# Layer-1 attention: normalise the probabilities on POOL before they are turned, one output product for a pair of heads

## The chip, the cores and the metric

One core of one Trainium2 chip runs the whole program. The metric is the device time of one execution in microseconds. The kernel before took 1533.4 us (median of three runs, 1531.64 to 1533.47). The engines are written as the profile writes them: PE is TensorE (with PEld for its weight loads), DVE is VectorE, ACT is ScalarE, POOL is GpSimd, SP is SyncE.

## The reference

The program computes a whole two-layer block on x of 2 x 1024 x 128: layer 0 has a test-time-training attention and a second attention with a mixture of experts; layer 1 has the causal attention below and a mixture of 8 experts with top 2. The change touches only the layer-1 attention: 16 heads of 64 dimensions, sequence 1024, batch 2.

```
k = einsum('ihd,bpd->biph', W_K, x)
q = einsum('ihd,bpd->biph', W_Q, x)
v = einsum('ihd,bpd->biph', W_V, x)
scores = einsum('biph,biqh->biqp', k, q)
mask = tril(ones((S, S)))
scores_masked = tril(scores) - 10000000000.0 * (1.0 - mask)
attn = softmax(scores_masked / sqrt(64), axis=-1)
z = einsum('biph,biqp->biqh', v, attn)
z_flat = transpose(z, (0, 2, 1, 3)).reshape(B, S, -1)
out = einsum('df,bqf->bqd', W_O, z_flat)
```

Its result is added to x, together with that of the experts.

## The kernel before

The attention stage runs from about 794 us (first projections) to 1375 us (first product of the experts). It works in 16 **rounds**; a round is one pair of heads of one batch element. Within a round `u` from 0 to 15 names a row tile `i = u // 2` of 128 queries and a head `h = u % 2` of the pair; the tile has `i + 1` blocks of 128 keys, so a row of probabilities has 128 to 1024 columns. Because all four engines work on different steps at once, the order of each is written out as a list of short words. A word with `'` belongs to the round before the current one, a word with `+` to the next. The words are:

- PE: `q k v` projections of 512 columns (L2044, L2052); `S` scores of one `u`, from the split parts KA, KB and QA (L2002, L2003); `T` turns (transposes) the probabilities of one `u`, up to four blocks at a time (L2010); `pv` multiplies them with V for one of three groups of tiles (0 to 3, 4 and 5, 6 and 7; L2024); `w` is the output product (L2037).
- DVE: `mx` masks the scores and takes the row minimum of their negative, in two records (L1516); `ql` writes the low part of Q, two operations with both inputs in SBUF (L1552); `kd` copies the high part of K to the other half of the partitions, two operations (L1555); `x` adds the output product to X (L1560, L1568); `gate` is the routing of the experts.
- ACT: `ex` is the exponential of a row, with its sum into SM (L1023).
- `tc`, `zc`, `vc`, `qr`, `kr` move results of PE out of PSUM, on ACT or DVE as the lists say.
- POOL: `qh`, `kh` write the high parts of Q and K (two casts each, L836, L842), `kl` the low part of K (two subtractions, L848).

PN holds the probabilities of three `u` at a time (`NPROB`), so `ex` of `u` waits for the turning of `u - 3`. S waits for the exponential that frees its PSUM banks: from `u = 10` that is `u - 2`. The ring of three PSUM banks takes the results of `T`, `w`, `q`, `k`, `v` in PE's order; each waits until the third one before it has been moved out.

The probabilities stay undivided until the very end. Z1 holds, for 128 queries, both heads of the pair in its 128 partitions (64 each). The sums of the two heads differ, so the output product is made per head: WOZ holds each head's 64 rows of W_O with zeros in the other 64, `w` makes four products of 128 columns (two tiles, two heads), and `x` multiplies each with 1/sum of its row and adds it to X. WOZ is cleared on POOL after `kl1` of the first round (L853) and filled by two DMAs. A round has 16 such products on PE, and 4 reciprocals of 4 columns and 16 multiply-adds of 128 columns on DVE. Before the first round POOL does, in this order, `kh1 kl1`, the clearing, `qh1 kh0 qh0 kl0`, and S0 waits for `ql0`, `kd0` and `kl0`.

Of the kernel before, what the change touches and what calls it, by code (L numbers as in the profile page):

```python
# [11 lines left out]
ALU = mybir.AluOpType  # L12
# [66 lines left out]
def program(nc, x_in, w0_in, w1_in, out):  # L79
    with ExitStack() as ctx:  # L80
# [123 lines left out]
        WOZ = sb("WOZ", [P, H1, D])  # L204
        NPROB = 3
# [253 lines left out]
        PAIRS = range(0, TB, 2)  # L459
# [18 lines left out]
        PE1 = steps1("T14.1' S0 T13.1' S1 T13.0' T15.0' w0' S2 T14.0' S3 T15.1' S4 k1+ T0.0 S5 k0+ S6 T1.0 w4' S7 T3.0 "  # L478
                     "T2.0 pv2' T5.0 T4.0 T6.0 S8 q1+ T7.0 S9 w2' q0+ S10 T8.0 T8.1 S11 pv0 T9.0 T9.1 S12 T11.1 T10.1 "
                     "v1 S13 v0+ T10.0 T11.0 S14 gate0+ T12.0 w6' T12.1 S15 pv1")  # L480
        DVE1 = steps1("gate1 mx5 x4' mx7 tc2.0 tc5.0 tc4.0 mx8 tc7.0 mx9 x2' mx10 mx11 ql0+ mx12 vc1 mx13 tc10.0 mx14 "
                     "gate0+ kd0+ mx15 x6' tc12.1 kd1+ mx1+ mx0+ x0 zc1 mx2+ mx3+ ql1+ mx4+ mx6+")
        ACT1 = steps1("tc13.1' tc13.0' tc15.0' ex0 ex1 tc14.0' tc15.1' gate0 ex2 kr1+ tc0.0 ex3 kr0+ tc1.0 ex4 tc3.0 "
                     "ex6 ex5 ex7 tc6.0 qr1+ ex8 ex9 zc2' qr0+ tc8.1 tc8.0 ex10 ex11 tc9.0 tc9.1 tc11.1 tc10.1 ex12 "
                     "vc0+ tc11.0 ex13 zc0 tc12.0 ex14 ex15 tc14.1")
        POOL1 = steps1("kh1 kl1 qh1 kh0 qh0 kl0")

        def rounds(steps):
# [10 lines left out]
        score_max, low_q, dup_k, out_added = (  # L499
            sem("l1_max"), sem("l1_q_low"), sem("l1_k_doubled"), sem("l1_out_added"))  # L500
# [4 lines left out]
        high_q, high_k, low_k = sem("l1_q_high"), sem("l1_k_high"), sem("l1_k_low")  # L505
# [4 lines left out]
        def counts(steps, **signals):  # L510
            n = {}
            for item, r in rounds(steps):
                if item[0] == "gate":
                    continue
                s = signals[item[0]]
                if item[0] == "x":
                    for part in ("r", 0, 1, 2):
                        n[s.name] = n.get(s.name, 0) + 1
                        done1[("x", item[1], part), r] = (s, n[s.name])
# [149 lines left out]
        def _(sp):  # L669
# [25 lines left out]
        def _(pool):  # L695
# [160 lines left out]
            after(pool, POOL1[-1][0], ROUNDS - 1)  # L856
            after(pool, ("kl", 0), ROUNDS - 1)
            after(pool, ("qh", 1), ROUNDS - 1)
# [22 lines left out]
        def _(act):  # L881
# [132 lines left out]
            for item, r in rounds(ACT1):  # L1014
# [17 lines left out]
                elif kind == "zc":  # L1032
                    g = item[1]
                    after(act, ("pv", g), r)
                    for i in PAIRS:
                        if GROUP_OF[i] == (g + 1) % 3:
                            after(act, ("w", i), r - 1 if g < 2 else r)
# [30 lines left out]
        def _(dve):  # L1068
# [436 lines left out]
            for item, r in rounds(DVE1):  # L1505
# [644 lines left out]
```

## Time and profile before

| | |
|---|---|
| median of three runs | 1533.4 us |
| the profiled execution | 1532.58 us |
| its span | 1530.8 us |
| PE busy | 1412.0 us (92%) |
| DVE busy | 1097.4 us (72%) |
| ACT busy | 786.8 us (51%) |
| POOL busy | 239.9 us (16%) |
| one round in the middle (1054.14 to 1088.21) | 34.07 us |

The shares are averages over all stages. What counts for this change is the stretch from 794 to 1375 us. A matrix product of f32 by f32 leaves two records on PE and its records overlap, so the pace of PE is read from the starts of successive groups and not from the durations.

### The profile page before, as it was taken

To read this page: it belongs to the slowest core of one execution; us is meant where nothing else is said; L and a number is where in the kernel's file an instruction comes from. 1 tells how busy PE (TensorE), PEld (TensorE's weight loads), DVE (VectorE), ACT (ScalarE), POOL (GpSimd) and SP (SyncE) were. 2 spreads that over 40 slices of the span, in tenths; PEclk is the share of its full clock that TensorE was granted. 3 is DMA by queue.
4 is the path that set the end of the run, shared out by engine and by line. 5 is a ranking of instruction groups with operands and counts; after the bars stand their busy time and mean duration, and the time that the engine had idled before them with its cause. 6 is when DMAs were issued, how large, how long until landed. Compare 5 with 4: busy or idle time off the path is not lost.

```text
span 1530.8 us, 30652 instructions
## 1 busy us (share of the span) xinstructions
PE 1412.0 (92%) x9716; PEld 1083.2 (71%) x9716; DVE 1097.4 (72%) x3133; ACT 786.8 (51%) x1701; POOL 239.9 (16%) x353
## 2 busy tenths in 40 slices
PE   4189999999899999979967999999999999989998
PEld 2167776777677787655645777777877777768887
DVE  3688887888788888463336788788878787855555
ACT  3315454555445464534334676666676776632332
POOL 4000000000000000000024233233222232400000
PEclk9599999999999999989997999999999999989999
DMA  2000000000000000030000000000000000000000
GB/s 95 0 1 1 2 2 3 2 2 2 3 2 2 1 2 1 1 138 1 0 0 15 1 1 2 1 1 2 1 1 1 1 1 1 1 1 1 0 0 27
DMA packets 5640, 12.35 MB, mean 8 GB/s; under 512 B 112, under 2 KB 5232, under 8 KB 5232
## 3 DMA queue, kind: packets, MB, share of 16 engines
q1 hardware_dynamic: 5488, 10.44, 1.9%
q8 instruction: 81, 1.33, 0.4%
q14 instruction: 71, 0.58, 0.1%
HBM read 9.39 MB, written 1.05 MB: 7 GB/s over the span
## 4 chain that ended last, share of the span: by engine, by line
PE 86%; DVE 7%; issue 4%; POOL 2%; ACT 1%; DVEq 0%; POOLq 0%; ACTq 0%
PE PS L1643 15%; PE PS L2010 9%; PE PS L2024 8%; PE PS L2078 6%; PE PS L1851 5%; PE PS L1828 5%; PE PS L2003 5%; PE PS L2002 4%; PE PS L1951 4%; PE PS L1869 4%; PE PS L2091 4%; PE PS L2037 4%; PE PS L2044 4%; PE PS L1813 2%; PE PS L1971 2%
## 5 line engine op out<-in xcount | busy, mean ns | idle before, releaser
L956 ACT ACTIVATE pe_<-PS 128x512 f32<-128x512 f32 (+3 forms) x384 | 177.8, 489 | 185.8 <-PE PS L1854 139.9
L1023 ACT ACTIVATE PN<-PS,NM 128x128 f32<-128x128 f32 (+7 forms) x256 | 189.7, 742 | 107.1 <-DVE NM L1516 52.9
L1516 DVE CUSTOM_DVE_ANT_0 PS<-PS,mask_row 128x128 f32<-128x128 f32 (+7 forms) x256 | 192.5, 773 | 44.4 <-PE PS L2003 40.4
L2002 PE MATMUL PS<-KA,QA 128*128 128x512 f32 (+3 forms) x384 | 162.1, 422 | 15.2 <-DVE KA L1555 14.4
L2010 PE MATMUL PS<-ident,PN 128*128 128x128 f32 x1152 | 171.4, 276 | 1.6 <-ACT PN L1023 1.5
L1851 PE MATMUL PS<-qtb,kta 128*128 128x512 f32 (+3 forms) x384 | 147.0, 411 | 8.1 <-issue 7.2
L1828 PE MATMUL PS<-kta,qta 128*128 128x512 f32 (+3 forms) x384 | 150.4, 420 | 4.4 <-DVE NMH L1329 2.3
L2010 PEld LDWEIGHTS PS<-ident,PN 128*128 128x128 f32 x1152 | 132.3, 141 | 27.7 <-issue 17.6
L1329 DVE TENSOR_REDUCE NMH<-PS 128x1 f32<-128x512 f32 (+3 forms) x256 | 144.2, 584 | 6.9 <-PE PS L1828 3.1
L2003 PE MATMUL PS<-KB,QA 128*128 128x512 f32 (+3 forms) x384 | 129.3, 349 | 0.0
L1851 PEld LDWEIGHTS PS<-qtb,kta 128*128 128x128 f32 x384 | 72.7, 196 | 38.3 <-ACT pe_ L956 21.4
L2002 PEld LDWEIGHTS PS<-KA,QA 128*128 128x128 f32 x384 | 73.9, 193 | 34.0 <-DVE QA L1552 14.5
L2078 PE MATMUL PS<-QA,w_s 128*128 128x512 f32 x256 | 83.6, 408 | 5.4 <-DVE w_s L1581 5.2
L848 POOL TENSOR_TENSOR KB<-RAW,KA 64x512 fp32r<-64x512 f32 x64 | 87.1, 1361 | 4.4
L1828 PEld LDWEIGHTS PS<-kta,qta 128*128 128x128 f32 x384 | 74.3, 196 | 18.3 <-issue 9.8
L842 POOL CAST KA<-RAW 64x512 fp32r<-64x512 f32 x64 | 46.2, 722 | 244.5 <-ACT RAW L1045 242.1
L2003 PEld LDWEIGHTS PS<-KB,QA 128*128 128x128 f32 x384 | 74.2, 193 | 12.8 <-issue 7.3
L1062 ACT ACTIVATE pe_<-PS 128x512 f32<-128x512 f32 x64 | 38.0, 599 | 86.3 <-PE PS L2078 56.0
L1869 PE MATMUL PS<-pe_,arena 128*32 128x512 f32 (+3 forms) x768 | 81.8, 498 | 0.0
L1031 ACT ACTIVATE PTB<-PS 128x512 f32<-128x512 f32 (+2 forms) x144 | 64.8, 483 | 31.1 <-PE PS L2010 30.0
L1031 ACT ACTIVATE pe_<-PS 128x512 f32<-128x512 f32 (+3 forms) x144 | 64.9, 483 | 26.3 <-PE PS L2010 25.1
L1552 DVE TENSOR_TENSOR QA<-RAW,QA 64x512 fp32r<-64x512 f32 x64 | 66.2, 1034 | 17.0 <-POOL QA L836 15.6
(258 smaller groups left out, 3160.7 us busy)
## 6 DMA issues: line engine op xcount, KB each, us to landing
W<-w SPq DMA_DIRECT2D x1, 5124.0 KB, 15.7
W<-w SPq DMA_DIRECT2D x1, 2508.0 KB, 11.1
X<-x SPq DMA_DIRECT2D x2, 512.0 KB, 4.8
out<-X SPq DMA_DIRECT2D x1, 1024.0 KB, 5.1
WOZ<-w SPq DMA_DIRECT2D x2, 256.0 KB, 4.1
```

The source lines that it names most:

```text
L956: act.activation(pe_[:, h, n % 2, 0:w], PS[:, 4 + h % 2, 0:w], ACT.Exp, scale=HD0 ** -0.5)\
L1023: act.activation(prob_rows(u, r), scores_of(u), ACT.Exp, bias=NM[:, u:u + 1], scale=-1.0, accum_out=SM[:, r % 2, u:u + 1]).then_inc(score_ ...
L1329: dve.tensor_reduce(dst, PS[:, 2 + r[1] % 2, 0:min(512, (i + 1) * P - 512 * k)], AX.X, ALU.max, negate=True).then_inc(f0_dve.sem, 1)
L1516: dve.tensor_tensor_reduce(scores_of(u), scores_of(u), mask_row[:, S - w:S], -HD1 ** -0.5, -MASKED, ALU.add, ALU.min, NM[:, u:u + 1]).then ...
L1643: return pe.matmul(*args, skip_group_check=True, **kw)
L1828: ins = pe.matmul(PS[:, bank, 0:w], qta[:, h, i * P:(i + 1) * P], kta[:, b, 512 * k:512 * k + w], start=True, stop=True)
L1851: ins = pe.matmul(PS[:, 4 + h % 2, 0:w], kta[:, 1 - b, j * P:(j + 1) * P], qtb[:, h, q0:q0 + w], start=True, stop=True)
L1869: ins = pe.matmul(PS[32 * h:32 * h + 32, 6, q0 - 512 * c:512], tmv[:, j, 32 * h:32 * h + 32], pe_[:, h, n % 2, 0:512 * (c + 1) - q0], star ...
L2002: pe.matmul(piece, query, KA[:, b, h, lo:lo + n], start=True, stop=False)
L2003: ins = pe.matmul(piece, query, KB[:, b, h, lo:lo + n], start=False, stop=True)
L2010: ins = pe.transpose(PS[:, ring_bank[item, r], (j - 4 * k) * P:(j - 4 * k + 1) * P], prob_rows(u, r)[:, j * P:(j + 1) * P], ident[:, :])
L2078: ins = pe.matmul(PS[:, 2 * (u % 3) + a, :], w[:, k, part, half * P:(half + 1) * P], xs[:, cols], start=(i == 0), stop=(i == 2))
```

## The change

`ex` now is followed by `rs` on DVE, the reciprocal of one column of sums, and by `nm` on POOL, which multiplies the row of probabilities in PN with it in place. `T` waits for `nm` and no longer for `ex`. Both heads of Z1 are then divided, so one product with the plain 128 rows of W_O serves both: `w` is there once per group of tiles and makes one product per tile, 8 in a round. `x` becomes one addition per group (512, 256 and 256 columns). WOZ, its clearing and its two DMAs are gone. PN holds four `u`. All four lists are written anew.

```
-        WOZ = sb("WOZ", [P, H1, D])
-        NPROB = 3
+        NPROB = 4
...
-        POOL1 = steps1("kh1 kl1 qh1 kh0 qh0 kl0")
+        POOL1 = steps1("nm11' nm12' nm13' nm14' qh0+ kh1 nm15' nm0 nm1 kl1 kh0+ nm3 nm2 nm4 kl0+ nm5 nm6 nm7 nm8 qh1+ "
+                     "nm9 nm10")
...
-            sp.wait_ge(wo_zero, 1)
-            pairs = WOZ[:, :, :].rearrange("p (m h) n -> p h m n", h=2)
-            lo, hi = W1_AT["wo"]
-            for h in range(2):
-                rows = slice(h * HD1, (h + 1) * HD1)
-                sp.dma_start(pairs[rows, h, :, :], w1_in[rows, lo:hi].rearrange("p (m n) -> p m n", n=D))\
-                    .then_inc(wo_loaded, 16)
...
+            before = None
             for item, r in rounds(POOL1):
                 kind = item[0]
-                if kind == "gate":
+                if before is not None and (kind == "nm") != (before[0][0] == "nm"):
+                    after(pool, *before)
+                before = item, r
+                if kind == "nm":
+                    u = item[1]
+                    after(pool, ("rs", u), r)
+                    pool.tensor_scalar(prob_rows(u, r), prob_rows(u, r), RS[:, u:u + 1], None, ALU.mult)\
+                        .then_inc(normed, 1)
                     continue
...
-                if (item, r) == (("kl", 1), 0):
-                    after(pool, ("kl", 1), 0)
-                    pool.memset(WOZ[:, :, :], 0.0).then_inc(wo_zero, 1)
-                    pool.wait_ge(wo_zero, 1)
...
                 elif kind == "x":
                     i = item[1]
+                    n = len(GROUPS[GROUP_OF[i]])
                     after(dve, ("w", i), r)
-                    dve.reciprocal(RS[:, 2 * i:2 * i + 4], SM[:, r % 2, 2 * i:2 * i + 4]).then_inc(out_added, 1)
-                    after(dve, ("x", i, "r"), r)
                     after(dve, ("x", i), r - 2)
-                    for n in range(4):
-                        h, t = n // 2, i + n % 2
-                        if h:
-                            after(dve, ("x", i, n - 2), r)
-                        xs = X[:, TB * (r % 2) + t, :]
-                        dve.scalar_tensor_tensor(xs, PS[:, ring_bank[("w", i), r], n * D:(n + 1) * D],
-                                                 RS[:, 2 * t + h:2 * t + h + 1], xs, ALU.mult, ALU.add)\
-                            .then_inc(out_added, 1)
+                    xs = X[:, TB * (r % 2) + i:TB * (r % 2) + i + n, :]
+                    dve.tensor_tensor(xs, PS[:, ring_bank[("w", i), r], 0:n * D].rearrange("p (t n) -> p t n", t=n), xs,
+                                      ALU.add).then_inc(out_added, 1)
+                elif kind == "rs":
+                    u = item[1]
+                    after(dve, ("ex", u), r)
+                    dve.reciprocal(RS[:, u:u + 1], SM[:, r % 2, u:u + 1]).then_inc(sum_inverse, 1)
...
                 elif kind == "T":
                     _, u, k = item
-                    after(pe, ("ex", u), r)
+                    after(pe, ("nm", u), r)
...
-                    for n in range(4):
-                        h, t = n // 2, i + n % 2
-                        ins = pe.matmul(PS[:, ring_bank[item, r], n * D:(n + 1) * D], Z1[:, half_of(g, r), columns(t)],
-                                        WOZ[:, 2 * hp + h, :], start=True, stop=True)
+                    at = W1_AT["wo"][0] + hp * P
+                    for t in GROUPS[g]:
+                        ins = pe.matmul(PS[:, ring_bank[item, r], (t - i) * D:(t - i + 1) * D], Z1[:, half_of(g, r), columns(t)],
+                                        W1[:, at:at + P], start=True, stop=True)
```

The lists move work in two places that matter below. The first is POOL at the start of the stage. The rows give the operations in program order with what they wait for; `l1_raw_by_act` is the copy of a projection out of PSUM, `l1_k_high` the end of a `kh`. Before:

```order
L824 MEMSET KB 64x2x1024 [waits pool_chain] x2
L842 CAST KA<-RAW 64x512 [waits l1_raw_by_act,pool_chain]
L842 CAST KA<-RAW 64x512
L848 ISA
L848 TENSOR_TENSOR KB<-RAW,KA 64x512 [waits l1_k_high]
L848 TENSOR_TENSOR KB<-RAW,KA 64x512
L853 MEMSET WOZ 128x2048 [waits l1_k_low]
L836 CAST QA<-RAW 64x512 [waits l1_raw_by_act,wo_rows_cleared]
L836 CAST QA<-RAW 64x512
L842 CAST KA<-RAW 64x512 [waits l1_raw_by_act]
L842 CAST KA<-RAW 64x512
```

And now:

```order
L811 MEMSET KB 64x2x1024 [waits pool_chain] x2
L831 CAST QA<-RAW 64x512 [waits l1_raw_by_act,pool_chain]
L831 CAST QA<-RAW 64x512
L837 CAST KA<-RAW 64x512 [waits l1_raw_by_act]
L837 CAST KA<-RAW 64x512
L843 ISA
L843 TENSOR_TENSOR KB<-RAW,KA 64x512 [waits l1_k_high]
L843 TENSOR_TENSOR KB<-RAW,KA 64x512
```

The first K and Q parts written are now those of columns 0 to 511 (`qh0 kh0 kl0`), which S0 reads; before they were the last of the stretch, behind `kh1 kl1`, the clearing and `qh1`.

The second place is DVE at the end of the first round, from the minima of its last rows (1024 columns) to the first minimum of the next round (128 columns). Before, from the second of the two minima on:

```order
L1516 ISA PS,NM<-PS,mask_row 128x1024 [waits l1_scores]
L1516 ISA NM 128x1
L1524 COPY pe_<-PS 128x3x128 [waits l1_pv,l1_turned]
L1555 COPY KA<-KA 64x512 [waits l1_k_high]
L1555 COPY KA<-KA 64x512
L1516 ISA PS,NM<-PS,mask_row 128x128 [waits l1_scores]
```

And now, from ahead of the first of the two:

```order
L1552 RECIPROCAL RS<-SM 128x1
L1536 TENSOR_TENSOR QA<-RAW,QA 64x512 x2
L1502 ISA PS,NM<-PS,mask_row 128x1024
L1502 ISA NM 128x1
L1552 RECIPROCAL RS<-SM 128x1
L1510 COPY PTB<-PS 128x2x128
L1539 COPY KA<-KA 64x512 x2
L1552 RECIPROCAL RS<-SM 128x1
L1502 ISA PS,NM<-PS,mask_row 128x1024
L1502 ISA NM 128x1
L1536 TENSOR_TENSOR QA<-RAW,QA 64x512 x2
L1502 ISA PS,NM<-PS,mask_row 128x128
```

Both pairs that write the low part of Q now stand here, one ahead of the first minimum of 1024 columns and one behind the second; reciprocals, which wait for ACT, stand between them, and one of the two copies of K as before.

## Rows read from the trace of the kernel before

**Rows 1.** Stretches: us, each engine's busy us (instructions), granted clock, DMA share, GB/s.
```profile
812.90:820.50 7.60, 7.34 (x19) 4.92 (x20) 4.25 (x14) 2.57 (x11) 1.76 (x3) 0.52 0.00 1
1054.14:1088.21 34.07, 34.07 (x249) 26.90 (x248) 27.32 (x69) 23.45 (x59) 10.83 (x12) 1.00 0.01 1
...
1355.30:1375.40 20.10, 13.49 (x112) 10.25 (x111) 16.56 (x57) 4.88 (x10) 0.00 (x0) 0.92 0.00 1
```

**Rows 2.** Waits of PE, 820 to 1355 us: total us, times, longest.
```profile
PE PS L2010 <- ACT PN L1023: 1.5, 1, 1.5
```

**Rows 3.** The same view, 798 to 820 us.
```profile
PE PS L2002 <- DVE KA L1555: 14.4, 1, 14.4
```

**Rows 4.** Timeline of PE, parts of two rounds: start us, us, line, operation, count.
```profile
1062.24 1.07 PE L2044 MATMUL PS<-XT,W 128*128 128x512 f32 x2
1063.15 0.60 PE L2010 MATMUL PS<-ident,PN 128*128 128x128 f32 x4
...
1074.80 1.04 PE L2010 MATMUL PS<-ident,PN 128*128 128x128 f32 x8
1075.59 0.48 PE L2002 MATMUL PS<-KA,QA 128*128 128x512 f32 x1
...
1076.61 0.60 PE L2010 MATMUL PS<-ident,PN 128*128 128x128 f32 x4
1077.04 1.06 PE L2037 MATMUL PS<-WOZ,Z 128*128 128x128 f32 x8
1077.93 0.49 PE L2010 MATMUL PS<-ident,PN 128*128 128x128 f32 x3
...
1083.90 1.06 PE L2037 MATMUL PS<-WOZ,Z 128*128 128x128 f32 x8
1084.71 0.36 PE L2002 MATMUL PS<-KA,QA 128*128 128x256 f32 x1
```

**Rows 5.** Groups by line, whole span: count, busy us, mean ns, idle before it.
```profile
L1568 DVE SCALAR_TENSOR_TENSOR X<-PS,RS,X 128x128 f32<-128x128 f32 x256 | 72.1, 344 | 2.7 <-DVE RS L1560 0.5
...
L1560 DVE RECIPROCAL RS<-SM 128x4 f32<-128x4 f32 x64 | 11.2, 175 | 19.0 <-PE PS L2037 18.2
...
L1398 DVE TENSOR_TENSOR X<-PS,X 128x512 f32<-128x512 f32 x4 | 2.5, 683 | 0.0
```

**Rows 6.** The same by shape, 813 to 1373 us: POOL with two inputs, then one.
```profile
L866 POOL TENSOR_TENSOR KA<-XT,QA 128x512 fp32r<-128x512 f32 x4 | 5.4, 1376 | 0.0
...
L862 POOL CAST QA<-XT 128x512 fp32r<-128x512 f32 x4 | 2.3, 616 | 8.2 <-PE PS L2003 8.2
```

**Rows 7.** Timeline of all engines at the start of the attention stage.
```profile
798.62 1.26 POOL L842 CAST KA<-RAW 64x512 fp32r<-64x512 f32 x2
...
808.46 2.93 POOL L848 TENSOR_TENSOR KB<-RAW,KA 64x512 fp32r<-64x512 f32 x2
808.49 3.45 DVE L1552 TENSOR_TENSOR QA<-RAW,QA 64x512 fp32r<-64x512 f32 x2 [15.59 <-POOL QA L836]
811.97 1.75 DVE L1555 CAST KA<-KA 64x512 fp32r<-64x512 f32 x4
...
812.92 0.44 PE L2002 MATMUL PS<-KA,QA 128*128 128x128 f32 x1 [14.37 <-DVE KA L1555]
...
815.20 0.69 PE L2002 MATMUL PS<-KA,QA 128*128 128x384 f32 x1 [0.23 <-ACT PN L1023]
```

**Rows 8.** Timeline of DVE: the two pairs of `ql` in one round.
```profile
1069.21 2.69 DVE L1552 TENSOR_TENSOR QA<-RAW,QA 64x512 fp32r<-64x512 f32 x2
...
1087.47 1.39 DVE L1552 TENSOR_TENSOR QA<-RAW,QA 64x512 fp32r<-64x512 f32 x2
```

**Rows 9.** Groups by shape, 813 to 1373 us: minimum and exponential of 1024 columns.
```profile
L1516 DVE CUSTOM_DVE_ANT_0 PS<-PS,mask_row 128x1024 f32<-128x1024 f32 x32 | 39.4, 1233 | 20.5 <-PE PS L2003 20.4
...
L1023 ACT ACTIVATE PN<-PS,NM 128x1024 f32<-128x1024 f32 x32 | 36.0, 1125 | 20.9 <-DVE NM L1516 20.9
```

More of the change, by code:

```diff
@@ L458, in program @@
         GROUP_OF = {i: g for g, tiles_ in enumerate(GROUPS) for i in tiles_}
-        PAIRS = range(0, TB, 2)
         S_BANK = [u % 4 if u < 8 else 2 * (u % 2) for u in range(2 * TB)]
@@ L476, in steps1 @@
             return steps
[L478 to L485, printed above, removed]
-        POOL1 = steps1("kh1 kl1 qh1 kh0 qh0 kl0")
+        PE1 = steps1("T11.1' k1 T12.1' gate0 q0+ S0 T13.0' T13.1' S1 pv1' T12.0' T14.0' k0+ S2 T14.1' S3 T15.0' S4 "
+                     "T15.1' S5 w4' T1.0 S6 T0.0 pv2' S7 T2.0 T3.0 S8 w0' v0+ T4.0 S9 T5.0 q1+ S10 T6.0 S11 v1+ T7.0 "
+                     "w6' S12 T8.0 S13 T9.0 T8.1 T9.1 pv0 S14 T10.1 T11.0 T10.0 S15")
+        DVE1 = steps1("gate1 mx4 rs2 mx3 mx5 kd1 rs3 rs4 x4' mx6 mx7 rs5 mx8 x0' rs6 vc0+ mx9 rs7 rs8 tc5.0 mx10 mx11 "
+                     "rs9 vc1+ x6' tc7.0 mx12 rs10 tc8.1 rs11 mx13 rs12 ql0+ mx14 rs13 tc11.1 kd0+ rs14 mx15 gate0+ "
+                     "ql1+ mx1+ mx0+ rs15 tc14.0 rs1+ mx2+ rs0+")
+        ACT1 = steps1("tc10.1' tc11.0' tc10.0' ex14' kr1 tc12.1' zc0' qr0+ tc13.1' ex15' tc13.0' ex1 zc1' tc12.0' ex0 "
+                     "kr0+ tc14.1' ex2 tc15.0' tc15.1' gate0 ex4 tc1.0 ex3 tc0.0 ex5 tc2.0 tc3.0 ex6 ex7 zc2' tc4.0 "
+                     "ex8 ex9 qr1+ tc6.0 ex10 ex11 tc8.0 tc9.1 ex12 tc9.0 ex13")
+        POOL1 = steps1("nm11' nm12' nm13' nm14' qh0+ kh1 nm15' nm0 nm1 kl1 kh0+ nm3 nm2 nm4 kl0+ nm5 nm6 nm7 nm8 qh1+ "
+                     "nm9 nm10")
         def rounds(steps):
@@ L498, in program @@
             sem("l1_scores"), sem("l1_turned"), sem("l1_pv"), sem("l1_out_products"), sem("l1_qkv_products"))
-        score_max, low_q, dup_k, out_added = (
-            sem("l1_max"), sem("l1_q_low"), sem("l1_k_doubled"), sem("l1_out_added"))
+        score_max, low_q, dup_k, out_added, sum_inverse = (
+            sem("l1_max"), sem("l1_q_low"), sem("l1_k_doubled"), sem("l1_out_added"), sem("l1_sum_inverse"))
         score_exp = sem("l1_exp")
@@ L515, in counts @@
                 s = signals[item[0]]
[L516 to L519, printed above, removed]
                 n[s.name] = n.get(s.name, 0) + 1
@@ L850, in _ @@
                     ins.then_inc(low_k, 1)
-                if (item, r) == (("kl", 1), 0):
-                    after(pool, ("kl", 1), 0)
-                    pool.memset(WOZ[:, :, :], 0.0).then_inc(wo_zero, 1)
-                    pool.wait_ge(wo_zero, 1)
-            after(pool, POOL1[-1][0], ROUNDS - 1)
-            after(pool, ("kl", 0), ROUNDS - 1)
-            after(pool, ("qh", 1), ROUNDS - 1)
+            after(pool, *before)
             after(pool, ("S", 15), ROUNDS - 2)
@@ L1034, in _ @@
                     after(act, ("pv", g), r)
-                    for i in PAIRS:
-                        if GROUP_OF[i] == (g + 1) % 3:
-                            after(act, ("w", i), r - 1 if g < 2 else r)
+                    after(act, ("w", GROUPS[(g + 1) % 3][0]), r - 1 if g < 2 else r)
                     dst, src = z_to(g, r)
@@ L1527, in _ @@
                     after(dve, ("pv", g), r)
-                    for i in PAIRS:
-                        if GROUP_OF[i] == (g + 1) % 3:
-                            after(dve, ("w", i), r - 1 if g < 2 else r)
+                    after(dve, ("w", GROUPS[(g + 1) % 3][0]), r - 1 if g < 2 else r)
                     dst, src = z_to(g, r)
@@ L2057, in _ @@
                     gate(1, w1("gate"), E1, ring_bank[item, r])
-            after(pe, ("x", PAIRS[-1]), ROUNDS - 1)
+            for group in GROUPS:
+                after(pe, ("x", group[0]), ROUNDS - 1)
             with pe.Fori(0, E1 // 2) as ep:
```

14 lines of the change are left out of this document (6 added, 8 removed).

## The prediction

> **What bounds the kernel now.** I read the stretches first. In a round in the middle of the stage PE is busy for all of its 34.07 us, at full granted clock, while DVE has 27.32, ACT 23.45 and POOL only 10.83 [rows 1]. The waits say the same from the other side: from 820 to 1355 us, almost all of 16 rounds, PE waits once, for 1.5 us [rows 2]. So work taken from PE in a round shortens the round, as long as what it then needs comes in time. The one large wait of PE in the stage is at its start: 14.4 us before the first scores [rows 3]. The timeline shows the chain there: POOL works through its list from 798.62 on, its last item `kl0` and DVE's `ql0` begin at 808.46 and 808.49, `kd` follows at 811.97, PE starts at 812.92 [rows 7]. Any change in the order of POOL's first items moves this start.
>
> **The products removed.** Records of products overlap, so I take starts: one `w` before (four products) holds PE from 1077.04 to 1077.93 and another from 1083.90 to 1084.71, 0.89 and 0.81 us, mean 0.85, which is 0.2125 us per product [rows 4]. A round goes from 16 to 8 products, 16 rounds lose 128: 128 x 0.2125 = 27.2 us, all on the path by the first paragraph. The round should become 34.07 - 1.70 = 32.37 us. The weight rows come from W1 instead of WOZ, which is the same operand shape and costs nothing.
>
> **The start.** POOL now begins with `qh0 kh0 kl0`. From 798.6: a pair of casts 1.26, another 1.26 (the row is that of `kh`; I take the same for `qh`), the subtractions 2.93 with the other engine beside them, and some 0.15 between: done at 804.2 [rows 7]. DVE's `ql0` starts when `qh0` ends (799.9) and takes 3.45 at worst, and half of the 1.75 for `kd0` follows: 804.3. So S0 can start at 804.3 rather than 812.9, 8.6 us earlier. But DVE's list has `ql1` ahead of the first minima, and S4 needs an exponential. `qh1` ends at 804.2 + 1.3 = 805.5, `ql1` takes 1.39 alone to 3.45 at worst [rows 7, 8], the minima and exponentials of two small rows some 1.5 (S0 to S4 took 2.3 in all before): S4 at 808.4 to 810.5 against 815.20 [rows 7], 4.7 to 6.8 earlier. By then PE has done three more projections than before (`k1`, `q0` and `k0` of the next round), each 0.91 [rows 4], 2.7 us of work that is not left over: 7.4 to 9.5 in all. I take 8. The clearing of WOZ and its DMAs also go; they were inside this chain and are counted with it. The granted clock was 0.52 for the 7.6 us behind the long wait [rows 1]; if it does not fall after the shorter one, up to 0.48 x 7.6 = 3.6 us more come back, if it falls as before, none. I take none and keep the other end.
>
> **POOL.** 16 `nm` in a round have 2 x (128 + 256 + ... + 1024) = 9216 columns. No row shows this operation. The nearest is the cast, one SBUF tensor in and one out: 616 ns for 512 columns, 1.20 ns per column with its fixed part; from above it is bounded by the subtraction with two tensors in, 1376 ns or 2.69 per column [rows 6]. That is 11.1 or 24.8 us per round, beside the 10.83 of before. `nm` reads one tensor and a single column, so I take the cast: 21.9 of 32.37 us. An `nm` of 1024 columns then takes about 1.2 us. The lists leave room for it: between S15 and `T15.0` PE has 24 blocks of other T at 0.10 (eight took 0.79) and three projections at 0.91 [rows 4], 5.1 us without `pv1` and the small S, while minimum, exponential [rows 9], reciprocal (at most 0.175 [rows 5]) and `nm` take 1.23 + 1.13 + 0.18 + 1.2 = 3.7. PN's fourth place gives back the distance that the two extra stages take.
>
> The Trainium skill speaks against the move: its page "GPSIMD Engine Reference", section "Performance versus the Vector engine", calls GpSimd the wrong choice for ordinary elementwise work, about half as fast as VectorE, but for one-input operations its section "When to use GPSIMD" says roughly line rate. By the latter an estimate from the page's 1.03 cycles per element at 1.2 GHz is 7.9 us per round plus fixed parts, which would leave the sum as it is; the 616 ns of [rows 6] agree with it.
>
> **DVE.** Per round it loses 16 multiply-adds of 344 ns and 4 reciprocals of 175, 6.2 us, and gains one addition of 683 and two of half the size (0.4 each, estimated from it), 1.5, and 16 reciprocals of at most 0.175, 2.8 [rows 5]: 27.3 - 1.9 = 25.4 of 32.37. It isn't the bound. But each `rs` waits for an exponential and holds up all that is behind it, and DVE now has a busy neighbour. One `ql` pair takes 1.39 us alone and 2.69 in the stretch where POOL subtracts [rows 8]. The tightest link that I find is `mx14`, `ex14`, S0 of the next round. Between the end of S14 and S0 PE has 10 blocks of T at 0.10 (eight took 0.79), S15 with 1.02, 5 blocks, and two projections with 0.91 [rows 4]: 4.3 us. `mx14` and `ex14` take 1.23 + 1.13 and some 0.3 for reading the accumulators: 2.7 [rows 9]. The slack is 1.6 us, and `ql0` and `rs12` sit ahead of `mx14`. Without a collision nothing is lost, with one 1.3 of the 1.6 is used. Some rounds will lose something: I take 0.3 us per round, 5 us in all, between nothing and 0.7 per round (11 us).
>
> For the collisions the Trainium skill ("SBUF — State Buffer", section "Who interferes with whom") has an exclusive lock: a VectorE operation with two SBUF inputs, or a copy in a two-port mode, and a GpSimd operation that reads SBUF never share; the second one waits for the whole of the first. By it every `ql` and `kd` pair can wait for a full `nm`, and the sum would move toward the first rival below; the 2.69 against 1.39 of [rows 8] agree with it.
>
> **The end of the stage.** The routing now stands on DVE behind the last probabilities, ahead of the last three `x`, and POOL stages the experts' input only after the last `nm`. From the last scores to the first expert product it was 20.1 us, with PE busy for 13.49 of them [rows 1]. Both moved pieces fill time in which PE waited; I take 0, with 2 us to either side.
>
> **Sum.** The profiled execution took 1532.6 us. 1532.6 - 27.2 - 8 + 5 + 0 = 1502.4, call it **1502**. The profiled execution is 0.8 below the median of 1533.4, less than a run differs from another. Own range: 27.2 + 12.2 + 2 gives 1491 at best; 27.2 + 4.7 - 11 - 2 gives 1514.
>
> **Rivals.**
>
> *Collisions on every link.* The four pairs of `ql` and `kd` now nearly always meet an `nm`. For it: POOL goes from 32% to 68% of a round, and DVE's list has both `ql` pairs and a `kd` next to the longest `nm`. Against: DVE keeps 7 us of air. Price: if the slack of 1.6 is used up and 1.3 us per round (one more collision) is lost, 16 x 1.3 = 21 in place of 5: 1518.
>
> *POOL becomes the bound (slower than before).* If `nm` costs what the subtraction costs, POOL has 10.83 + 24.8 = 35.6 us per round, more than the 34.07 of before. 16 x (35.6 - 34.07) = 25, less 8 at the start: 1532.6 + 25 - 8 = 1549. It decides from 21.5 us of `nm` per round, 2.3 ns per column, and turns the whole into a loss from 23.7 us (the round then is 34.07 + 8/16), 2.6 ns per column. For it: no row of this operation, and a scalar from memory as second operand. Against: that is one column, not a second tensor.
>
> *The clock falls inside the rounds.* The clock is full in all middle rounds, where PE never waits, and was 0.52 for 7.6 us behind a 14.4-us wait [rows 1, 3]. If each round now had a wait long enough for that, it would lose 3.6 us more beside the wait: at 1 us of wait, 16 x 4.6 = 74 in place of 5: 1571. Against: it takes waits of PE that the slack above does not give, and the middle rounds start from a full clock [rows 1].
>
> **Chances.** Forecast 0.67, collisions 0.20, POOL bound 0.08, clock 0.05. The range that should hold 8 of 10 is 1491 to 1522, which takes in the collisions. A measurement of this kernel tells 0.2% (3 us) from no change. Faster by more: 0.86, from the first two cases; within it: 0.03, a POOL price between its ends; slower: 0.11.
>
> **What would show it.** PE: 128 fewer products, 8 per round, a round of 32.4 to 32.7 us, and no wait above 0.7 us in it. `nm` at about 1.2 us for 1024 columns and 0.3 for 128; from 2.3 ns per column on the forecast is wrong. S0 at about 804 and S4 near 809 (a wait of PE on DVE in between). Under the first rival PE's waits name exponentials, with `mx` late behind `ql`; under the second PE waits for `nm` and POOL shows no idle time; under the third the stretches show a granted clock below 1 in the middle.

## The result

The changed kernel takes 1602.18 us (median of four runs, 1598.28 to 1603.26) against 1532.52 for the kernel before (median of four, 1530.97 to 1533.47): ratio 1.0451, 95% interval 1.0429 to 1.0472. It is 70 us slower; 1502 was predicted. The profiled execution is the shortest of the four: 1598.28 us, span 1596.5. It is 65.7 us longer than that of the kernel before, and this difference is what the traces can account for.

### The profile after

A middle round, as in [rows 1] (us, then busy us and instructions of PE, PEld, DVE, ACT, POOL, then the granted clock):

```profile
1100.67:1139.24 38.57, 33.68 (x234) 25.16 (x233) 25.83 (x66) 24.04 (x59) 37.48 (x28) 1.00 0.00 1
```

The round is 38.57 us instead of 34.07. PE is busy for only 33.68 of them and POOL for 37.48. The only wait of PE of any size, from 820 to 1420 us, is the one for `nm` (as [rows 2]):

```profile
PE PS L1993 <- POOL PN L822: 69.6, 70, 1.9
```

The group of `nm` over the whole span, and two of its shapes (count, busy us, mean ns, idle before; as [rows 5, 6]):

```profile
L822 POOL TENSOR_SCALAR PN<-PN,RS 128x128 f32<-128x128 f32 (+7 forms) x256 | 437.3, 1727 | 13.5 <-DVE RS L1552 8.0
```

```profile
L822 POOL TENSOR_SCALAR PN<-PN,RS 128x1024 f32<-128x1024 f32 x30 | 85.4, 2847 | 1.4
...
L822 POOL TENSOR_SCALAR PN<-PN,RS 128x128 f32<-128x128 f32 x32 | 19.0, 606 | 0.1
```

From 606 ns for 128 columns to 2847 for 1024 each column costs 2.50 ns, on top of 0.29 us per instruction. The prediction had taken 1.20 ns per column in all, with 2.69 as its upper end. The 16 `nm` of a round take 437.3 / 16 = 27.3 us; 11.1 was taken and 24.8 was the bound. With 10.2 us of the other POOL work and 1.1 of gaps that is the 38.57. POOL's timeline of this round shows what a bound engine looks like, one group behind another with only hand-overs between them:

```profile
1100.67 1.26 POOL L831 CAST QA<-RAW 64x512 fp32r<-64x512 f32 x2
1102.03 14.08 POOL L822 TENSOR_SCALAR PN<-PN,RS 128x640 f32<-128x640 f32 x6
1116.17 1.26 POOL L831 CAST QA<-RAW 64x512 fp32r<-64x512 f32 x2
1117.49 1.27 POOL L837 CAST KA<-RAW 64x512 fp32r<-64x512 f32 x2
1118.85 4.01 POOL L822 TENSOR_SCALAR PN<-PN,RS 128x1024 f32<-128x1024 f32 x3
1122.94 2.60 POOL L843 TENSOR_TENSOR KB<-RAW,KA 64x512 fp32r<-64x512 f32 x2
...
1132.98 6.19 POOL L822 TENSOR_SCALAR PN<-PN,RS 128x384 f32<-128x384 f32 x4
```

That the price is the operation's own and not the neighbour's is seen in how little it varies. Of all 256 `nm` the shortest took 603 ns and the longest 2853 (the first three numbers are shortest, median and longest); these are, within 0.5%, the means of 128 and of 1024 columns above. So no `nm` was held up, whatever DVE did beside it.

```profile
L822 POOL TENSOR_SCALAR PN<-PN,RS x256: 603/1730/2853, 810.5 to 1422.6; 128x128 f32<-128x128 f32 x16, 128x256 f32<-128x256 f32 x16, 128x384 f32<-128x384 f32 x16, 128x512 f32<-128x512 f32 x16
```

`ql` on DVE was hardly held up either. Here one `nm` of 1024 columns runs from 1073.88 to 1076.73, and a whole pair of `ql`, whose operations read two SBUF tensors, starts and ends inside it, in 1.72 us against 1.39 for a pair alone [rows 8]:

```profile
1073.88 2.85 POOL L822 TENSOR_SCALAR PN<-PN,RS 128x1024 f32<-128x1024 f32 x1
1074.51 1.72 DVE L1536 TENSOR_TENSOR QA<-RAW,QA 64x512 fp32r<-64x512 f32 x2
```

S0 and S4 came as the prediction had it (compare [rows 7]): POOL's first pairs are `qh0 kh0 kl0`, S0 begins at 805.70 instead of 812.92, `ql1` stands ahead of the first minima, and S4 comes at 809.90 instead of 815.20.

```profile
799.10 1.26 POOL L831 CAST QA<-RAW 64x512 fp32r<-64x512 f32 x2
...
800.40 1.70 DVE L1536 TENSOR_TENSOR QA<-RAW,QA 64x512 fp32r<-64x512 f32 x2 [0.59 <-POOL QA L831]
800.42 2.15 POOL L837 CAST KA<-RAW 64x512 fp32r<-64x512 f32 x2
...
802.67 2.89 POOL L843 TENSOR_TENSOR KB<-RAW,KA 64x512 fp32r<-64x512 f32 x2
...
805.70 0.45 PE L1985 MATMUL PS<-KA,QA 128*128 128x128 f32 x1 [4.90 <-POOL KB L843]
...
806.91 1.70 DVE L1536 TENSOR_TENSOR QA<-RAW,QA 64x512 fp32r<-64x512 f32 x2 [2.48 <-POOL QA L831]
...
809.90 0.66 PE L1985 MATMUL PS<-KA,QA 128*128 128x384 f32 x1 [0.44 <-ACT PN L1011]
```

The sum of the 65.7 us goes by stretches between the same points in both profiled executions: S0, the exponential of the last row (`ex15`) of the first round, the same of the round before the last, and that of the last. Before, then now (columns as in the middle round above):

```profile
812.92:842.39 29.47, 27.70 (x153) 20.45 (x155) 22.12 (x47) 18.73 (x49) 10.34 (x12) 0.88 0.01 1
842.39:1319.29 476.90, 476.90 (x3474) 376.68 (x3472) 381.48 (x948) 328.53 (x798) 152.94 (x171) 1.00 0.01 1
1319.29:1356.71 37.42, 36.78 (x264) 30.59 (x262) 24.90 (x65) 21.02 (x52) 8.76 (x10) 0.91 0.01 1
```

```profile
805.70:842.40 36.70, 30.18 (x148) 22.22 (x150) 24.46 (x62) 19.37 (x49) 35.31 (x29) 0.80 0.00 1
842.40:1386.54 544.14, 477.27 (x3250) 358.91 (x3248) 360.10 (x925) 335.90 (x812) 524.79 (x393) 0.98 0.00 1
1386.54:1421.14 34.60, 32.31 (x242) 25.09 (x240) 20.25 (x61) 21.84 (x56) 32.43 (x21) 1.00 0.00 1
```

S0 is 7.2 us earlier, but the rest of the first round takes 7.2 us more, with POOL busy for 35.3 of its 36.7 us: at its end nothing of the start is left. The next 14 rounds take 67.2 us more, which is 14 x 4.5 = 63.0 and 4.2 on top. The last takes 2.8 less, and the way from there to the first product of the experts 1.5 more (20.28 against 18.74). That makes 66.0.

Of the 4.2 us 3.9 come from five rounds of 39.1 to 39.5 us instead of 38.6. Their mean granted clock is 0.96: in each it was at the lower of its two levels, 1.2 instead of 2.4 GHz, for 3.4 us, about 1 us after PE had waited 1.9 us for an `nm`. One of these rounds, and the stretch in it:

```profile
881.00:920.50 39.50, 35.10 (x236) 26.67 (x234) 25.43 (x67) 24.06 (x60) 37.51 (x29) 0.96 0.00 1
888.90:892.30 3.40, 3.40 (x15) 2.99 (x13) 2.78 (x9) 0.98 (x2) 3.20 (x4) 0.50 0.00 0
```

PE waited these 1.9 us at the same place in all 14 rounds (1.93 to 888.00 in this one, 1.93 to 849.40 in the one before, where the clock stayed at 1.00). Why the clock fell after five of them stays open.

The first product of the experts begins at 1441.42 against 1375.45, 66.0 later; from there to the end of the span both kernels need the same 155 us.

```profile
1441.42 1.19 PE L2060 MATMUL PS<-QA,w_s 128*128 128x512 f32 x2 [8.22 <-DVE w_s L1564]
```

### The profile page after: what moved, and what is told of

The parts are those of the page before. It is cut to its first block and busy times, and to the rows that moved or that the text cites. A ratio compares the mean times of both kernels' runs of the same rounds, so it can differ in the third digit from the quotient of the medians.

```text
span 1596.5 us, 30438 instructions
## 1 busy us (share of the span) xinstructions
PE 1410.2 (88%) x9460; PEld 1061.7 (66%) x9460; DVE 1072.7 (67%) x3101; ACT 795.8 (50%) x1717; POOL 666.1 (42%) x608
## 5 line engine op out<-in xcount | busy, mean ns | idle before, releaser
L822 POOL TENSOR_SCALAR PN<-PN,RS 128x128 f32<-128x128 f32 (+7 forms) x256 | 437.3, 1727 | 13.5 <-DVE RS L1552 8.0
L944 ACT ACTIVATE pe_<-PS 128x512 f32<-128x512 f32 (+3 forms) x384 | 177.8, 489 | 186.1 <-PE PS L1837 140.2
L1993 PE MATMUL PS<-ident,PN 128*128 128x128 f32 x1152 | 179.6, 281 | 73.6 <-POOL PN L822 73.6
L1985 PE MATMUL PS<-KA,QA 128*128 128x512 f32 (+3 forms) x384 | 165.8, 432 | 7.8 <-POOL KB L843 4.9
L769 POOL COPY arena<-arena 128x256 f32 (+1 forms) x8 | 3.2, 403 | 281.3 <-PE PS L1852 281.3
L1019 ACT ACTIVATE PTB<-PS 128x512 f32<-128x512 f32 (+3 forms) x152 | 73.7, 496 | 89.1 <-PE PS L1993 87.5
L1019 ACT ACTIVATE pe_<-PS 128x512 f32<-128x512 f32 (+3 forms) x152 | 73.9, 496 | 88.0 <-PE PS L1993 86.6
L843 POOL TENSOR_TENSOR KB<-RAW,KA 64x512 fp32r<-64x512 f32 x64 | 81.8, 1279 | 4.5
```

The lines of the kernel that those rows point to most:

```text
L822: pool.tensor_scalar(prob_rows(u, r), prob_rows(u, r), RS[:, u:u + 1], None, ALU.mult)\
L944: act.activation(pe_[:, h, n % 2, 0:w], PS[:, 4 + h % 2, 0:w], ACT.Exp, scale=HD0 ** -0.5)\
L1019: act.activation(dst, src, ACT.Copy).then_inc(turned_a, 1)
L1985: pe.matmul(piece, query, KA[:, b, h, lo:lo + n], start=True, stop=False)
L1993: ins = pe.transpose(PS[:, ring_bank[item, r], (j - 4 * k) * P:(j - 4 * k + 1) * P], prob_rows(u, r)[:, j * P:(j + 1) * P], ident[:, :])
```

## The experiments

All are made from the changed kernel, except the one on the start. Ratios are to the kernel before on the same chip: 1530.38 us beside the copy, the constant, the start and the four longest rows on DVE, 1531.00 beside half of the columns, every second row, all rows on DVE and the product of two tensors, 1530.43 beside the last three. The theory (A): POOL's product with a scalar costs 2.5 ns per column, POOL is the bound, and everything else of the forecast holds. Its rival (B): the extra hops from ACT over DVE and POOL to PE, and the access that POOL shares with DVE, stretch everything, whatever the operation.

### A copy in place of the product

```
-                    pool.tensor_scalar(prob_rows(u, r), prob_rows(u, r), RS[:, u:u + 1], None, ALU.mult)\
+                    pool.tensor_copy(prob_rows(u, r), prob_rows(u, r))\
```

> The changed kernel with nm as a plain copy in place (PN to PN) on POOL; the division by the row sum is left out. Everything else, orders and waits too, is as changed. Theory A (price per column: nm took 2847 ns for 1024 columns and fills POOL, 37.48 of 38.57 us per round): a copy at the cast's 616 ns per 512 columns leaves POOL 10.2 + 11 = 21 us per round, PE is the bound again, round 32.4 to 32.8 us, total 1500 to 1508 us, PE waits less than 0.5 us per round for nm. Theory B (the extra hops from ACT over DVE and POOL to PE, and the ports that POOL shares with DVE, not the operation itself): the copy is stretched too and the round stays above 36 us, total 1560 to 1600.

Measured: 1498.06 us, ratio 0.9792 (0.9776 to 0.9809). A round, and the copy in two shapes:

```profile
1103.31:1135.67 32.36, 32.36 (x236) 25.29 (x234) 24.91 (x67) 23.82 (x59) 21.86 (x28) 1.00 0.00 1
```

```profile
L822 POOL COPY PN<-PN 128x1024 f32<-128x1024 f32 x32 | 33.3, 1040 | 29.8 <-DVE RS L1552 28.9
...
L822 POOL COPY PN<-PN 128x128 f32<-128x128 f32 x30 | 7.9, 290 | 16.0 <-DVE RS L1552 16.0
```

The hops, the waits, the order and the neighbours are all as in the changed kernel, and only the operation differs. The round becomes 32.36 us, PE is busy for all of it, and there is no wait of PE for POOL in the middle rounds. So B is out: the stages added cost nothing here. (The copy leaves out the division.) The copy costs 1.04 us for 1024 columns, 0.84 ns per column, and 1498.06 is within 0.3% of the 1502 that the prediction worked out from the price of a cast.

### A constant in place of the scalar from memory

```
-                    pool.tensor_scalar(prob_rows(u, r), prob_rows(u, r), RS[:, u:u + 1], None, ALU.mult)\
+                    pool.tensor_scalar(prob_rows(u, r), prob_rows(u, r), 0.5, None, ALU.mult)\
```

> The changed kernel with nm multiplying by the constant 0.5 in place of the value per row from RS; the division by the row sum is left out. If the scalar read from memory per row is what costs (theory A1), nm falls to the price of a cast, about 1.2 us for 1024 columns, and the time to 1500 to 1508 us. If the arithmetic operation as such costs it (theory A2), 1024 columns stay at 2.6 to 2.9 us and the time at 1590 to 1603.

Measured: 1574.58 us, one run, round 37.20. (The constant leaves out the division too.)

```profile
L822 POOL TENSOR_SCALAR PN<-PN 128x1024 f32<-128x1024 f32 x32 | 88.7, 2771 | 3.8 <-DVE RS L1552 2.5
...
L822 POOL TENSOR_SCALAR PN<-PN 128x128 f32<-128x128 f32 x32 | 16.4, 529 | 0.1
```

The column price is the same 2.50 ns; what a scalar from memory adds is 0.08 us per instruction. A1 is out for the column price. The expected time of A2 (1590 to 1603) was too high, because 16 x 0.08 = 1.3 us per round come back and POOL is the bound.

### The start alone, in the kernel before

```
+        FIRST = [(("qh", 0), 0), (("kh", 0), 0), (("kl", 0), 0), (("qh", 1), 0), (("kh", 1), 0), (("kl", 1), 0)]
...
+            if steps is POOL1:
+                yield from FIRST
             for slot in range(-1, ROUNDS + 1):
                 for item, late in steps:
+                    if steps is POOL1 and slot - late == 0:
+                        continue
```

> The kernel before with only POOL's first six items in another order: qh0 kh0 kl0 qh1 kh1 kl1, the clearing of WOZ last; all later rounds as before. The start term of the prediction alone: S0 at 805 to 806 us instead of 812.9, and 5 to 8 us off the total: 1525 to 1528. Rival: the wait only moves, to the scores of tile 4 that need the second half of K and Q or to the first output product that needs WOZ, and the total stays at 1530 to 1533.

Measured: 1523.64 us, ratio 0.9965 (0.9952 to 0.9977), 6.7 us less. S0 and S4:

```profile
804.72 0.45 PE L2007 MATMUL PS<-KA,QA 128*128 128x128 f32 x1 [6.45 <-DVE KA L1560]
...
810.10 0.69 PE L2007 MATMUL PS<-KA,QA 128*128 128x384 f32 x1 [3.34 <-ACT PN L1028]
```

S0 moves from 812.92 to 804.72 and PE then waits 3.3 us for the exponential ahead of S4, as the prediction had it for the changed kernel. The term of the start stands, but 8 was too much: in the trace `ex15` of the first round is 5.9 us earlier (836.45 against 842.39), and in the run with the copy, which has the whole new order, 6.3 (836.14). What this run has beyond 5.9 lies in the last round, where the trace of the kernel before had a granted clock of 0.91 and this one 1.00.

### Half of the columns

```
+                    pool.tensor_scalar(prob_rows(u, r)[:, 0:(u // 2 + 1) * P // 2], prob_rows(u, r)[:, 0:(u // 2 + 1) * P // 2],
+                                       RS[:, u:u + 1], None, ALU.mult)\
```

> The changed kernel with nm on POOL over only the first half of the columns of each row; the other half stays undivided. POOL's load of nm falls evenly from 27.3 to 16 x 0.29 + 4608 x 2.5 ns = 16.2 us, in all 26.4 per round, less than the 27.5 of the run with u = 12 to 15 moved (round 36.0). If only POOL's share of a round counted, both would have the same round, about 36; if it is how evenly it is spread (theory A), here the round is 32.4 to 33.2 and the time 1498 to 1512.

Measured: 1501.53 us, one run. The round is 32.62 us with POOL at 26.64:

```profile
1106.83:1139.45 32.62, 32.57 (x236) 25.36 (x234) 25.00 (x67) 23.81 (x60) 26.64 (x29) 1.00 0.00 1
```

The same operation at the same price, only half as much of it in every step, and PE is the bound again.

### The four longest rows on DVE

The next three runs, and two of the last ones, give a part or all of the divisions to DVE: each becomes a `nm` in DVE's list, right behind its `rs`, and goes from POOL's.

```
-                     ... rs11 mx13 rs12 ql0+ mx14 rs13 tc11.1 kd0+ rs14 mx15 gate0+ ql1+ mx1+ mx0+ rs15 tc14.0 ...
+                     ... rs11 mx13 rs12 nm12 ql0+ mx14 rs13 nm13 tc11.1 kd0+ rs14 nm14 mx15 gate0+ ql1+ mx1+ mx0+ rs15 nm15 tc14.0 ...
...
+                elif kind == "nm":
+                    u = item[1]
+                    after(dve, ("rs", u), r)
+                    dve.tensor_scalar(prob_rows(u, r), prob_rows(u, r), RS[:, u:u + 1], None, ALU.mult)\
+                        .then_inc(normed_v, 1)
```

> The changed kernel with the division of the four longest rows of a round (u = 12 to 15, 896 and 1024 columns) moved from POOL to DVE, each right behind its reciprocal; the other twelve stay on POOL. Result complete. Theory A (POOL's price): POOL loses 2 x (2.53 + 2.85) = 10.8 us per round, 37.5 to 26.7, and DVE gains 4 x 0.6 to 1.2 us (25.8 to 28.2 or 30.6): PE bounds again, round 32.4 to 33.5, total 1500 to 1520, faster than before. Theory B (hops and shared ports): DVE's and POOL's operations block each other more than before, round above 35, total above 1545.

Measured: 1554.02 us, ratio 1.0159 (1.0142 to 1.0176). The time lies in the range that was written for theory B, and theory A's 1500 to 1520 is missed. But the copy, with the same hops, has ruled B out, and the trace shows another reason. The round is 35.99 us, though POOL has only 27.50 of it:

```profile
1102.22:1138.21 35.99, 33.03 (x236) 25.17 (x234) 27.82 (x71) 23.81 (x60) 27.50 (x24) 1.00 0.01 2
```

```profile
1106.79 2.60 POOL L843 TENSOR_TENSOR KB<-RAW,KA 64x512 fp32r<-64x512 f32 x2
1109.49 6.18 POOL L822 TENSOR_SCALAR PN<-PN,RS 128x384 f32<-128x384 f32 x4
1115.74 1.26 POOL L831 CAST QA<-RAW 64x512 fp32r<-64x512 f32 x2
1117.10 6.24 POOL L822 TENSOR_SCALAR PN<-PN,RS 128x640 f32<-128x640 f32 x3
1128.62 1.26 POOL L831 CAST QA<-RAW 64x512 fp32r<-64x512 f32 x2 [5.27 <-ACT RAW L1031]
```

From 1102 to 1123 POOL goes without a gap through `nm3` to `nm11`, and PE waits for it there (44.2 us in all rounds); then it stands idle for 5.3 us, because what filled that part of its list was moved away. The half of the columns above had almost the same total, 26.64, evenly spread, and lost 0.3 us a round. So POOL's share of a round isn't what decides, but its load over each stretch of the list between the scores and their T.

### Every second row on DVE

```
-                     ... rs3 rs4 ... rs5 mx8 ... rs7 rs8 ... rs9 vc1+ ... rs11 mx13 ... rs13 tc11.1 ... rs15 tc14.0 rs1+ ...
+                     ... rs3 nm3 rs4 ... rs5 nm5 mx8 ... rs7 nm7 rs8 ... rs9 nm9 vc1+ ... rs11 nm11 mx13 ... rs13 nm13 tc11.1 ... rs15 nm15 tc14.0 rs1+ nm1+ ...
```

> The changed kernel with the division of every second row (u odd, head 1 of each tile) moved from POOL to DVE, behind its reciprocal; the even ones stay on POOL. Result complete. In the run with u = 12 to 15 moved, POOL had 27.5 us in a round of 36.0 and still was late for u = 0 to 11 (its list was full there and idle for 7.6 us at the end of the round). If that bunching is the cause (theory A), spreading the relief gives POOL some 24 us, evenly, DVE 25.8 + 8 x 0.2 + 4608 columns at 0.6 to 0.75 ns = 30 to 31 us, and the round falls to 32.4 to 33.5: 1498 to 1518 us. If instead DVE is now what is late (theory C, its operations wait for exponentials and for POOL's port), the round stays at 34 to 36: 1525 to 1555, with PE waiting on ACT (exponentials) rather than on nm.

Measured: 1504.41 us, ratio 0.9827 (0.9811 to 0.9844). It beats both kernels: it is 26.6 us below the one before on the same chip.

```profile
1109.07:1141.85 32.78, 32.69 (x236) 25.18 (x234) 29.47 (x75) 23.88 (x60) 25.16 (x20) 1.00 0.00 1
```

POOL has 25.16 us, little less than with the four longest rows moved, but spread, and the round is 32.78. PE has no wait of more than 1 us in the middle rounds. DVE is at 29.47.

### All rows on DVE

The same, with an `nm` behind all 16 `rs` and none on POOL.

> The changed kernel with all 16 divisions of a round on DVE and none on POOL. Result complete. POOL falls to about 10 us per round, DVE rises from 25.8 by 16 x 0.15 + 9216 columns at 0.55 to 0.75 ns = 7.5 to 9.3 us to 33 to 35 us, above the 32.35 of PE: DVE bounds, round 34 to 36.5, total 1525 to 1565. If DVE's price per column is much lower than with POOL beside it (theory C: the port was the cost), round 33, total 1505 to 1515.

Measured: 1522.43 us, ratio 0.9940 (0.9923 to 0.9957).

```profile
1113.83:1147.66 33.83, 33.19 (x235) 25.28 (x233) 32.89 (x84) 23.87 (x58) 11.06 (x13) 1.00 0.00 1
```

```profile
L1557 DVE TENSOR_SCALAR PN<-PN,RS 128x896 f32<-128x896 f32 x32 | 22.0, 687 | 1.4
...
L1557 DVE TENSOR_SCALAR PN<-PN,RS 128x512 f32<-128x512 f32 x32 | 15.6, 486 | 1.3
```

DVE takes 0.69 us for 896 columns and 0.52 ns per column between the two rows, nearly five times as fast as POOL (of the 1024 columns, 1.17 us on average, every second one met POOL's subtractions and took 1.68 us, the others 0.75). It is full now (32.89 of 33.83) and bounds the round, as expected, but 0.2 us below the expected 34 to 36.5, and the time is below the expected 1525. Even so the kernel is 0.6% faster than before.

### The product of two tensors on POOL

```
-                    pool.tensor_scalar(prob_rows(u, r), prob_rows(u, r), RS[:, u:u + 1], None, ALU.mult)\
+                    pool.tensor_tensor(prob_rows(u, r), prob_rows(u, r),
+                                       RS[:, u:u + 1].broadcast_to([P, (u // 2 + 1) * P]), ALU.mult)\
```

> The changed kernel with nm on POOL as a product of two tensors, the second one the column of RS repeated by its access pattern (step 0). Result complete. The subtraction of 512 columns with two inputs took 1376 ns, of which the fixed part is small: 1024 columns would take 2.4 to 2.7 us, no more than the 2.85 of the product with a scalar; round 36.5 to 38.5, 1568 to 1600 us. If the product with a scalar is slow for a reason of its own (theory A1), this form is faster than it by more than 10%; if the price is that of any arithmetic on POOL (A2), it is within 10%.

Measured: 1537.47 us, one run, round 34.82.

```profile
L822 POOL TENSOR_TENSOR PN<-PN,RS 128x1024 f32<-128x1024 f32 x32 | 60.6, 1893 | 20.1 <-DVE RS L1553 18.9
...
L822 POOL TENSOR_TENSOR PN<-PN,RS 128x128 f32<-128x128 f32 x32 | 12.1, 397 | 1.6 <-DVE RS L1553 1.6
```

A miss: 1.89 us for 1024 columns against 2.85 for the same values by `tensor_scalar`, 1.67 ns per column against 2.50. So the price is not that of arithmetic on POOL in general (A2 in its strict form falls); the one-tensor product is the dearer form. Here POOL no longer is the bound (29.34 of 34.82 us), and PE waits for the copy of K on DVE (`kd`) more than for `nm`:

```profile
PE PS L1986 <- DVE KA L1540: 17.1, 15, 2.1
PE PS L1994 <- POOL PN L822: 10.6, 14, 0.8
```

In this run a `ql` operation took 1442 ns on average (852 with half of the columns as `tensor_scalar`) and a `kd` 966 (752). The fast form gives back on DVE a part of what it saves on POOL. How it does so can be read in the timelines: the second `ql` of this pair began at 1041.28, inside an `nm` that ended at 1042.81, and it ended at 1043.35.

```profile
1040.68 2.13 POOL L822 TENSOR_TENSOR PN<-PN,RS 128x896 f32<-128x896 f32 x1
1039.85 3.50 DVE L1537 TENSOR_TENSOR QA<-RAW,QA 64x512 fp32r<-64x512 f32 x2
```

All 45 `ql` of the middle rounds that began inside an `nm` of this form ended 0.54 to 0.55 us after that `nm`, however long it still had. So they waited for its end and weren't merely slowed. In the changed kernel, with the product by a scalar, all 56 `ql` between 820 and 1370 us began and ended inside one `nm`, and none took more than 1.15 us. That form isn't free of meetings everywhere: with every second row on DVE a POOL `nm` of 896 columns begins 0.06 us after a `ql` in 15 rounds and takes 3.02 instead of 2.53 us, and the next `ql` 1.41.

### Even rows on POOL as products of two tensors

Both edits above together.

> The run with the odd rows divided on DVE (round 32.78 us, 1504.4 us), its even rows on POOL now as a product of two tensors (the column of RS repeated), which took 1.89 us for 1024 columns against 2.85. Result complete. Theory A (only POOL's load counts): POOL falls from 25.2 to about 20 us per round, round 32.4, 1497 to 1501 us. Theory C (POOL's two-input form holds up DVE: with it a ql operation took 1442 ns on average against 867): DVE, with 29.5 us per round already the fullest after PE, becomes late, round 33 to 34.5, 1508 to 1532 us.

Measured: 1523.57 us, ratio 0.9957 (0.9940 to 0.9973): 19 us worse than with the dearer operation. Round 33.99, POOL 21.09, DVE 31.08 instead of 29.47. PE's waits are for the copies of turned probabilities by DVE:

```profile
PE PS L2031 <- DVE pe_ L1511: 9.1, 7, 1.3
PE PS L2031 <- DVE PTB L1511: 9.1, 7, 1.3
```

`ql` went from 867 to 1265 ns on average. Less work on POOL made the kernel slower, through DVE: theory C held. All 30 `ql` that began inside an `nm` again ended 0.54 to 0.55 us after it.

### The copy of K earlier in DVE's list, twice

```
-                     ... rs9 vc1+ ... tc11.1 kd0+ rs14 ...
+                     ... rs9 kd0+ vc1+ ... tc11.1 rs14 ...
```

On the run with all divisions as products of two tensors:

> All divisions on POOL as products of two tensors (1537.5 us, round 34.82), and in DVE's list kd0 of the next round moved from behind mx14 to behind rs9. PE waited there 17.1 us for that kd and 10.6 for nm. If the wait is one of order (kd0 late behind ql0, mx14 and reciprocals), moving it returns most of the 17.1 us: 1518 to 1526. If DVE simply is held up by POOL wherever its operations stand (theory C), the wait moves to ql0 or the exponentials and the total stays at 1532 to 1538.

and on the run with every second row on DVE:

> The run with the odd rows divided on DVE (1504.4 us), with only kd0 of the next round moved in DVE's list from behind mx14 to behind rs9. Result complete. The round there is 32.78 us against 32.35 with a plain copy, 0.43 us or 7 us in all that DVE's lateness costs. If it is the end of DVE's round that is too full, 2 to 6 us come back: 1498 to 1502. If the place doesn't matter, 1503 to 1505.

Measured: 1550.96 (ratio 1.0135, 1.0118 to 1.0152) and 1522.12 us (0.9943, 0.9927 to 0.9960), 13.5 and 17.7 us worse. The wait for `kd` went, and another came, in the first of the two:

```profile
PE PS L1994 <- DVE VS L1529: 19.7, 15, 1.4
```

and in the second:

```profile
PE PS L1998 <- DVE VS L1528: 14.4, 14, 1.0
```

`VS` is `vc1`, which now stands behind `kd0`. It empties a bank of the ring of three. In PE's order `v1`, `T7.0`, `w6`, `T8.0` follow one another in the ring, so `T8.0` can't start without it; in a round of the first of the two runs it starts at 1114.08 after 1.4 us of waiting for `VS`. I had looked at `kd` and at `ql`, and at no item that the move pushed back.

## Why the prediction was wrong

**The products removed: right.** 27.2 us were taken, and the round should have been 32.37 us. With a copy for `nm` it is 32.36 (32.35 to 32.37 in 13 of the rounds).

**The start: right in its mechanism, 2 us too large.** S0 came at 805.7 (804.3 predicted), S4 at 809.9 (808.4 to 810.5 predicted). By the end of the first round it brought 5.9 us alone and 6.3 with the copy; 8 were taken. In the changed kernel it brought nothing, because POOL bound the first round too. That the clock would give nothing back there, as was taken, held: the granted clock from S0 to `ex15` was 0.80 against 0.88 before.

**POOL: wrong, and this decided.** The step of the prediction that failed is "`nm` reads one tensor and a single column, so I take the cast: 21.9 of 32.37 us". It took 11.1 us per round for `nm`, and 27.3 were measured; with them POOL had 37.5 us of work in a round for which the forecast gave PE 32.4, and POOL became the bound. Both ends of the bound were taken from operations of another kind. One-tensor-in is not a class of its own on POOL: the copy costs 0.84 ns per column, the product with a constant 2.50. Nor was the two-tensor subtraction an upper end: its 2.69 per column includes a fixed part and a result in another format, and the product by two tensors costs 1.67, less than the one-tensor product. The mechanism stood in the second rival, "POOL becomes the bound", with its turning point of 2.3 ns per column; it got a chance of 0.08 and a time of 1549 us. By the prediction's own terms 16 x 4.5 - 8 = 64 us more, and not 17, follow from the true price. A duration that no row showed was multiplied by 256 instructions, and the widest unknown of the sum got the narrowest tail of the range.

**One input.** "GPSIMD Engine Reference" of the Trainium skill speaks of roughly line rate for one-input operations in "When to use GPSIMD". The copy agrees with it (1.04 us for 1024 columns). The product with a scalar does not: 2.77 to 2.85 us. The measurement decides. Its warning against ordinary elementwise work on this engine was the better guide here.

**Collisions: nothing in the forecast form, real in others.** 5 us were taken; with the copy as `nm` PE lost nothing in the middle rounds, so the slack of 1.6 us at the end of a round was enough. They cost time when POOL runs the product of two tensors: `ql` took 1442 against 852 ns, and the whole kernel 19 us more when this form replaced the dearer one. The prediction's sentence that by the Trainium skill ("SBUF — State Buffer", "Who interferes with whom") every `ql` can wait for a full `nm` goes with the product of two tensors: there each `ql` that began inside an `nm` ended only after it. It does not hold for the form that the kernel uses: 56 of 56 `ql` ran inside a `tensor_scalar`, the second of each pair as fast as alone (686 to 690 ns). The measurement decides.

**The forecast as a whole, with a cheap `nm`: near, in part by luck.** The profiled run with the copy is 34.5 us below that of the kernel before, where 30.2 were forecast. The start brought 1.7 us less than taken and the collisions cost 5 less; the two errors go opposite ways.

**The clock: left out, and it cost 4 us.** It was 1.00 in most middle rounds, but five of the 14 had a stretch at half of it, for 0.5 to 0.9 us each. This is the third rival at a small part of its price: 3.6 us more in each of 16 rounds were written for it. In none of the other runs did the clock fall in a middle round.

**The end: right.** From the last `ex15` to the experts it took 1.5 us more, within the 2 that were allowed.

**What stays open.** The other three executions of the changed kernel took 3 to 5 us more than the profiled one; no trace shows where.

## What to carry to other kernels

A price that no row shows is to be measured before its place in the sum is trusted, and most of all on the engine that is to receive most of the work: here one run with the operation in place would have told 27 from 11. When work moves to an engine with room, compare its load in each stretch between producer and consumer, and not its share of a round: 27.5 us bunched lost 3.6 us a round against the copy's 32.36, 26.6 evenly spread lost 0.3. An item moved forward in a list that waits in order pushes others back; look at those first, above all at what empties a shared ring.

## What the runs showed of the hardware

On POOL, f32, 128 partitions, in place: copy 0.84 ns per column, product of two tensors with the second repeated 1.67, product with a scalar 2.50, whether the scalar is a constant or read per row (the latter adds 0.08 us per instruction). Why the form with one tensor is slower than that with two stays open. The same product on DVE took 0.52 ns per column, with no product on POOL beside it. A DVE operation of 64x512 with two SBUF inputs (686 ns alone) that began while POOL ran a product of two tensors ended 0.54 to 0.55 us after it; while POOL ran a product with a scalar, in the changed kernel, it took 0.69 to 1.15 us and didn't wait for the end. Why the two forms differ in this stays open too. Nothing in these runs tells whether the in-place form matters; it was not varied.
